# Starting the four TensorE lanes of a convolution loop one step apart instead of two

## The chip, the cores and the metric

One core of one Trainium2 chip runs the whole program. The metric is the device time of one execution in microseconds. All instructions are issued by hand on five engines: TensorE (PE in the profile, with its weight loads as PEld), VectorE (DVE), ScalarE (ACT), GpSimd (POOL) and SyncE (SP), which only starts transfers. Engines wait for each other by semaphores.

## The reference, cut to what matters

```python
# x: (32, 128, 2048) float32; cond_128: (32, 128)
def cond_1x1(x, embedding, ...):            # L0, L2 and L3
    att = softmax(mlp(embedding))           # 8 weights per batch element
    agg_w = einsum('bk,koi->boi', att, weight[..., 0])
    return einsum('boi,bih->boh', agg_w, x) + (att @ bias_k)[:, :, None]

def conv(x, c, weight, c_weight, bias):     # L1: 9 taps, 4 groups of 32 channels
    out = lax.conv_general_dilated(x, weight, (1,), [(4, 4)], feature_group_count=4, ...)
    return out + einsum('nd,od->no', c, c_weight)[:, :, None] + bias[None, :, None]

x = x + cond_1x1(x, cond_128, L0...)
x = x + conv(x, cond_128, L1..., fside_S_0)
x = x + cond_1x1(x, cond_128, L2...)
x = x + cond_1x1(x, cond_128, L3...)
```

## The kernel before, in words

The first 39 us prepare, for each of the 32 batch elements, one 128x128 matrix for L0 plus the identity, and one for the product of L2 and L3. The loop over the batch elements is then three stages, each with float32 data split in a high and a low part, so that every product is made of three matmuls (high by high, low by high, high by low):

- layer 0 (`layer0_steps`, matmuls at L479): x times the L0 matrix, into the four PSUM banks of `aux_ps`. ScalarE makes the high part of the result (`x1_hi`, L610), VectorE the low part (`x1_lo`, L767).
- the convolution (`conv_steps`, L499): into the four PSUM banks of `cv_ps`. ScalarE makes `x2_hi` (L618) and VectorE `x2_lo` (L776).
- the output product (`out_steps`, L522): into `aux_ps` again. ScalarE adds the bias and writes `y_all` (L628), and SyncE stores it.

VectorE also splits the next input (L758 and L751), GpSimd splits the next matrices (L693, L703). VectorE's order in a turn of the loop is x2_lo of the last element, x1_lo of the next, then the input split. ScalarE's is x2_hi, x1_hi, y.

Each stage exists four times, once for each group g of 32 rows of TensorE's array, and each copy writes a bank of its own. A lane is such a copy: lane g runs all stages of all elements with operands of the 32 partitions `rows(g)`. A step is one matmul of 32x512 of each lane. Layer 0 and the output product take 12 steps each in a lane, the convolution 36, so a turn of the loop is 60 steps or 240 matmuls. In a lane, a turn n is: layer 0 of element n+1 (12 steps), 18 steps of the convolution of n, the output product of n-1 (12 steps), the last 18 steps of the convolution of n. `in_turn` takes one matmul from each lane in the order 0, 1, 2, 3 and writes them in that one order into TensorE's queue. `LAG` is the number of steps by which each lane starts after the one ahead of it:

```python
def lane(g):
    for _ in range(LAG * g):
        yield
    ...
    for _ in range(LAST_WAIT - LAG * g):
        yield
    yield from out_steps(B - 1, g)
```

Before, lanes 1, 2 and 3 are 2, 4 and 6 steps behind lane 0. `LAST_WAIT` (5) holds lane 0 back ahead of the last output product, which needs all four lanes' results of the last convolution.

The waits that matter for the change stand at the start of each stage. `conv_steps(n, g)` (L493, L494) waits until VectorE has finished the `x1_lo` of all four lanes of element n, and until it has finished with this lane's own convolution bank, `x2_lo` of element n-1 in bank g. `out_steps(n, p)` (L511 to L518) waits for `x2_lo` of all four banks and for `x1_lo` of n+2 in bank p. `layer0_steps` (L470 to L477) waits for the split matrices, the split input and for y to have left bank p. A lane's bank of `cv_ps` is thus free between the end of one convolution and the start of the next only for the 12 steps of layer 0 between them, and in that time ScalarE and then VectorE have to read it.

Of the kernel before, what the change touches and what calls it, by code (L numbers as in the profile page):

```python
# [37 lines left out]
PER = PH // HALVES  # L38
YBUFS = 4
CONV_A = 18  # L40
LAG = 2
LAST_WAIT = 5


# [25 lines left out]
def cond_resid_kernel(nc, x, net, consts, mix, bias, conv, c_weight, w3, out):  # L70
    with ExitStack() as ctx:  # L71
# [304 lines left out]
        def _(pe):  # L376
# [132 lines left out]
            def out_steps(n, p):  # L509

                pe.wait_ge(m_split, 2 * (n + 1))  # L511
                pe.wait_ge(x2_lo_done, PH * (n + 1))


                if n + 2 < B:
                    pe.wait_ge(x1_lo_done, PH * (n + 2) + p + 1)
                elif n + 2 == B:
                    pe.wait_ge(y_out, PH * (n - 1) + p + 1)  # L518
                i, steps = 0, 3 * G
                for g in range(G):  # L520
                    for w, a in ((m_hi, x2_hi), (m_lo, x2_hi), (m_hi, x2_lo)):
                        mm = pe.matmul(out_bank(n, p), w[n % 2][rows(p), g, :], a[n % 2][rows(p), g, :],  # L522
                                       start=(i == 0), stop=(i == steps - 1))
                        i += 1
                        if i == steps:
                            mm.then_inc(y_done, 1)
# [6 lines that stand above are left out]
# [10 lines left out]
                yield from out_steps(B - 2, g)  # L543
                for _ in range(LAST_WAIT - LAG * g):
                    yield
# [368 lines left out]
```

## Time and profile before

| | us |
|---|---|
| median of 3 runs | 491.51 |
| lowest, highest | 489.49, 498.12 |
| the profiled execution's own time | 491.17 |
| its span in the profile | 489.0 |
| mean granted TensorE clock | 0.997 of full |

The span goes from the first to the last instruction of the profiled execution; its own time is 2.17 us longer. TensorE is busy for 478.8 us of the span, VectorE for 327.0, ScalarE for 252.7 and GpSimd for 150.8. The ends of matmuls in the profile are modelled, so the start of a matmul and the start of the ScalarE instruction that reads its bank are the firmer numbers.

### The profile page before, as it was taken

To read this page: it belongs to the slowest core of one execution; us is meant where nothing else is said; L and a number is where in the kernel's file an instruction comes from. 1 tells how busy PE (TensorE), PEld (TensorE's weight loads), DVE (VectorE), ACT (ScalarE), POOL (GpSimd) and SP (SyncE) were. 2 spreads that over 40 slices of the span, in tenths; PEclk is the share of its full clock that TensorE was granted. 3 is DMA by queue.
4 is the path that set the end of the run, shared out by engine and by line. 5 is a ranking of instruction groups with operands and counts; after the bars stand their busy time and mean duration, and the time that the engine had idled before them with its cause. 6 is when DMAs were issued, how large, how long until landed. Compare 5 with 4: busy or idle time off the path is not lost.

```text
span 489.0 us, 17826 instructions
## 1 busy us (share of the span) xinstructions
PE 478.8 (98%) x7953; PEld 475.4 (97%) x7953; DVE 327.0 (67%) x416; ACT 252.7 (52%) x417; POOL 150.8 (31%) x149
## 2 busy tenths in 40 slices
PE   6999999999999999999999999999999999999995
PEld 5989999999999999999999999999999999999995
DVE  3857767766687676666787676768777676777423
ACT  4654455544454555444554555445545554455435
POOL 3832441424332241433223141333143143330110
PEclk9999999999999999999999999999999999999998
DMA  8397996566657666564656656565767756552224
GB/s 264 139 311 205 320 269 217 163 205 164 186 158 212 218 214 214 166 201 129 184 194 217 215 184 204 130 207 155 217 208 216 211 157 198 146 184 64 88 88 172
DMA packets 39099, 92.84 MB, mean 190 GB/s; under 512 B 4584, under 2 KB 25584, under 8 KB 35056
## 3 DMA queue, kind: packets, MB, share of 16 engines
q1 hardware_dynamic: 39024, 91.71, 60.3%
q8 instruction: 63, 1.03, 0.9%
q14 instruction: 12, 0.10, 0.1%
HBM read 53.93 MB, written 37.77 MB: 188 GB/s over the span
## 4 chain that ended last, share of the span: by engine, by line
PE 95%; DVE 2%; DMA 1%; ACT 1%; SPq 0%; DVEq 0%; issue 0%; POOL 0%
PE cv_ps L499 56%; PE aux_ps L479 18%; PE aux_ps L522 17%; PE cv_ps L424 2%; DMA consts_sb<-in_consts_dram 1%; DVE x_lo L751 1%; PE aux_ps L424 1%; PE cv_ps L522 1%; DVE shares L796 1%; ACT x_hi L610 0%; DVE x_lo L767 0%; DVEq L71 0%; PE cv_ps L459 0%; ACT x_hi L601 0%; PE aux_ps L396 0%
## 5 line engine op out<-in xcount | busy, mean ns | idle before, releaser
L499 PE MATMUL cv_ps<-x_hi,conv_lo 32*128 32x512 f32 x1536 | 327.8, 391 | 0.0
L499 PE MATMUL cv_ps<-x_hi,conv_hi 32*128 32x512 f32 x1536 | 327.2, 389 | 0.0
L499 PE MATMUL cv_ps<-x_lo,conv_hi 32*128 32x512 f32 x1536 | 327.1, 391 | 0.0
L499 PEld LDWEIGHTS cv_ps<-x_hi,conv_lo 32*128 32x128 f32 x1536 | 240.4, 183 | 0.2 <-issue 0.2
L499 PEld LDWEIGHTS cv_ps<-x_lo,conv_hi 32*128 32x128 f32 x1536 | 240.2, 184 | 0.1
L499 PEld LDWEIGHTS cv_ps<-x_hi,conv_hi 32*128 32x128 f32 x1536 | 239.0, 183 | 0.0
L776 DVE SCALAR_TENSOR_TENSOR x_lo<-cv_ps,d_all,x_hi 128x512 fp32r<-128x512 f32 x128 | 87.2, 744 | 132.4 <-ACT x_hi L618 132.4
L628 ACT ACTIVATE y_all<-aux_ps,e_all 128x512 f32<-128x512 f32 x124 | 75.2, 690 | 134.4 <-PE aux_ps L522 134.4
L479 PE MATMUL aux_ps<-x_hi,a_hi 32*128 32x512 f32 x512 | 116.6, 391 | 0.5 <-DVE x_lo L751 0.5
L479 PE MATMUL aux_ps<-x_lo,a_hi 32*128 32x512 f32 x512 | 116.6, 389 | 0.0
L479 PE MATMUL aux_ps<-x_hi,a_lo 32*128 32x512 f32 x512 | 116.5, 388 | 0.0
L522 PE MATMUL aux_ps<-x_hi,m_hi 32*128 32x512 f32 x496 | 115.0, 387 | 0.0
L522 PE MATMUL aux_ps<-x_hi,m_lo 32*128 32x512 f32 x496 | 114.5, 387 | 0.0
L522 PE MATMUL aux_ps<-x_lo,m_hi 32*128 32x512 f32 x496 | 113.9, 384 | 0.0
L618 ACT ACTIVATE x_hi<-cv_ps,d_all 128x512 fp32r<-128x512 f32 x128 | 77.8, 687 | 66.7 <-PE cv_ps L499 66.7
L751 DVE TENSOR_TENSOR x_lo<-x_sb,x_hi 128x1024 fp32r<-128x1024 f32 x64 | 89.1, 1396 | 2.9 <-ACT x_hi L601 0.9
L767 DVE SCALAR_TENSOR_TENSOR x_lo<-aux_ps,c_all,x_hi 128x512 fp32r<-128x512 f32 x128 | 87.4, 746 | 4.8 <-ACT x_hi L610 2.9
L610 ACT ACTIVATE x_hi<-aux_ps,c_all 128x512 fp32r<-128x512 f32 x128 | 77.8, 691 | 18.1 <-PE aux_ps L479 18.1
L693 POOL CAST a_hi<-a_rep 128x512 fp32r<-128x512 f32 x32 | 24.4, 764 | 191.3 <-DMA a_rep<-a_pairs 126.3
L479 PEld LDWEIGHTS aux_ps<-x_hi,a_hi 32*128 32x128 f32 x512 | 78.6, 183 | 0.8 <-issue 0.6
L479 PEld LDWEIGHTS aux_ps<-x_hi,a_lo 32*128 32x128 f32 x512 | 78.8, 184 | 0.1
L479 PEld LDWEIGHTS aux_ps<-x_lo,a_hi 32*128 32x128 f32 x512 | 78.5, 183 | 0.2
(123 smaller groups left out, 538.1 us busy)
## 6 DMA issues: line engine op xcount, KB each, us to landing
x_sb<-in_x_dram SPq DMA_DIRECT2D x31, 1024.0 KB, 6.6
out_dram<-y_all SPq DMA_DIRECT2D x62, 512.0 KB, 7.4
a_rep<-a_pairs SPq DMA_DIRECT2D x64, 128.0 KB, 7.5
m_rep<-m_pairs SPq DMA_DIRECT2D x64, 128.0 KB, 7.0
a_pairs<-a_all SPq DMA_DIRECT2D x1, 1920.0 KB, 12.4
m_pairs<-m_all SPq DMA_DIRECT2D x1, 1792.0 KB, 12.6
m_all<-in_mix_dram SPq DMA_DIRECT2D x3, 512.0 KB, 5.2
x_sb<-in_x_dram SPq DMA_DIRECT2D x2, 512.0 KB, 7.5
```

Source lines behind the costliest of these rows:

```text
L424: mm = pe.matmul(mix_bank(n, h)[:, B * HO * i:B * HO * (i + 1)], w[half_rows(h), ROUND * j + i, :], a[half_rows(h)].rearrange("p b o -> p ...
L479: mm = pe.matmul(aux_ps[:, p, :], w[n % 2][rows(p), g, :], a[h][rows(p), g % PER, :], start=(i == 0), stop=(i == steps - 1))
L499: mm = pe.matmul(cv_ps[:, g, :], w[rows(g), j, :], a[n % 2][rows(g), q, s:s + T], start=(i == 0), stop=(i == steps - 1))
L522: mm = pe.matmul(out_bank(n, p), w[n % 2][rows(p), g, :], a[n % 2][rows(p), g, :], start=(i == 0), stop=(i == steps - 1))
L610: nc.scalar.activation(x1_hi[n % 2][:, p, 1:T + 1], aux_ps[:, p, :], ACT.Identity, bias=c0_all[:, n:n + 1]).then_inc(x1_hi_done, 1)
L618: nc.scalar.activation(x2_hi[n % 2][:, g, :], cv_ps[:, g, :], ACT.Identity, bias=d_all[:, g, n:n + 1]).then_inc(x2_hi_done, 1)
L628: nc.scalar.activation(y_all[:, k % YBUFS, p % PER, :], bank[:, p, :], ACT.Identity, bias=e_all[:, n:n + 1]).then_inc(y_out, 1)
L693: nc.gpsimd.tensor_copy(a0_hi[n % 2][:], src).then_inc(a0_split, 1)
L751: nc.vector.tensor_tensor(x_lo[h][:], x_sb[n % 2][:, PER * h:PER * (h + 1)], x_hi[h][:].bitcast(F32), ALU.subtract).then_inc(x_lo_done, 1)
L767: nc.vector.scalar_tensor_tensor(x1_lo[n % 2][:, p, 1:T + 1], aux_ps[:, p, :], c0_all[:, n:n + 1], x1_hi[n % 2][:, p, 1:T + 1].bitcast(F32 ...
L776: nc.vector.scalar_tensor_tensor(x2_lo[n % 2][:, g, :], cv_ps[:, g, :], d_all[:, g, n:n + 1], x2_hi[n % 2][:, g, :].bitcast(F32), ALU.add, ...
L796: nc.vector.tensor_scalar(shares[:], lexp[:].unsqueeze(1).unsqueeze(3).to_broadcast([NB, 2, K, HO]), linv[:], None, ALU.mult).then_inc(sha ...
```

## The change

`LAG` goes from 2 to 1. Lanes 1, 2 and 3 start 1, 2 and 3 steps after lane 0. No instruction is added or removed, no tile changes its size, and all waits have the same semaphores and values. The order of TensorE's queue is different, because matmuls of other lanes now stand beside each other. The order on the other engines is as it was. The waiting ahead of the last output product (`LAST_WAIT - LAG * g`) was 5, 3, 1 and 0 steps and is 5, 4, 3 and 2, so that lane 3 begins it in step with the others and no longer one step later.

```diff
-LAG = 2
+LAG = 1
```

TensorE's queue where the lanes go from layer 0 to the convolution of element 1, before. The row with `[waits x2_lo_done,x1_lo_done]` is the first convolution matmul of a lane; the first row here is that of lane 2 and the last that of lane 3.

```order
342 L499 MATMUL cv_ps<-x_hi,conv_hi 128x512 [waits x2_lo_done,x1_lo_done]
343 L479 MATMUL aux_ps<-x_hi,a_lo 128x512
344 L499 MATMUL cv_ps<-x_lo,conv_hi 128x512
345 L499 MATMUL cv_ps<-x_hi,conv_hi 128x512
346 L499 MATMUL cv_ps<-x_hi,conv_lo 128x512
347 L479 MATMUL aux_ps<-x_lo,a_hi 128x512
348 L499 MATMUL cv_ps<-x_hi,conv_hi 128x512
349 L499 MATMUL cv_ps<-x_hi,conv_lo 128x512
350 L499 MATMUL cv_ps<-x_lo,conv_hi 128x512
351 L499 MATMUL cv_ps<-x_hi,conv_hi 128x512 [waits x2_lo_done,x1_lo_done]
```

The same place of TensorE's queue now, with the first convolution matmuls of lanes 0, 1 and 2.

```order
331 L499 MATMUL cv_ps<-x_hi,conv_hi 128x512 [waits x2_lo_done,x1_lo_done]
332 L479 MATMUL aux_ps<-x_lo,a_hi 128x512
333 L479 MATMUL aux_ps<-x_hi,a_lo 128x512
334 L479 MATMUL aux_ps<-x_hi,a_hi 128x512
335 L499 MATMUL cv_ps<-x_hi,conv_lo 128x512
336 L499 MATMUL cv_ps<-x_hi,conv_hi 128x512 [waits x2_lo_done,x1_lo_done]
337 L479 MATMUL aux_ps<-x_lo,a_hi 128x512
338 L479 MATMUL aux_ps<-x_hi,a_lo 128x512
339 L499 MATMUL cv_ps<-x_lo,conv_hi 128x512
340 L499 MATMUL cv_ps<-x_hi,conv_lo 128x512
341 L499 MATMUL cv_ps<-x_hi,conv_hi 128x512 [waits x2_lo_done,x1_lo_done]
```

From one lane's first convolution matmul to the next lane's there were 9 places in the queue (two steps of four, and one), and now there are 5 (one step of four, and one).

## Rows read from the trace of the kernel before

**Rows 1.** Page, part 1: engine, busy us (share of the span), instructions.
```profile
PE 478.8 (98%) x7953; PEld 475.4 (97%) x7953; DVE 327.0 (67%) x416; ACT 252.7 (52%) x417; POOL 150.8 (31%) x149
```

**Rows 2.** Page, part 4: the chain that ended last, by engine.
```profile
PE 95%; DVE 2%; DMA 1%; ACT 1%; SPq 0%; DVEq 0%; issue 0%; POOL 0%
```

**Rows 3.** Waits of PE, all: line waited for, us in total, times, longest us.
```profile
PE aux_ps L396 <- DVE shares L796: 2.3, 1, 2.3
PE cv_ps L406 <- DVE idle_sb L786: 1.2, 1, 1.2
PE aux_ps L382 <- DMA m_rep<-in_net_dram: 0.8, 1, 0.8
PE aux_ps L479 <- DVE x_lo L751: 0.5, 1, 0.5
PE cv_ps L457 <- DVE c_att L826: 0.4, 1, 0.4
```

**Rows 4.** Timeline of DVE, 260 to 275 us: start, us, what [idle before <-releaser].
```profile
260.27 2.73 DVE L776 SCALAR_TENSOR_TENSOR x_lo<-cv_ps,d_all,x_hi 128x512 fp32r<-128x512 f32 x4 [3.29 <-ACT x_hi L618]
...
274.20 2.73 DVE L776 SCALAR_TENSOR_TENSOR x_lo<-cv_ps,d_all,x_hi 128x512 fp32r<-128x512 f32 x4 [4.47 <-ACT x_hi L618]
276.99 2.73 DVE L767 SCALAR_TENSOR_TENSOR x_lo<-aux_ps,c_all,x_hi 128x512 fp32r<-128x512 f32 x4
```

**Rows 5.** Timeline of ACT, 273 to 280 us.
```profile
273.48 2.42 ACT L618 ACTIVATE x_hi<-cv_ps,d_all 128x512 fp32r<-128x512 f32 x4 [1.68 <-PE cv_ps L499]
276.27 2.42 ACT L610 ACTIVATE x_hi<-aux_ps,c_all 128x512 fp32r<-128x512 f32 x4 [0.37 <-PE aux_ps L479]
```

**Rows 6.** Timeline of PE, 273.0 to 273.3 us: lane 0 ends its convolution.
```profile
273.04 0.39 PE L499 MATMUL cv_ps<-x_lo,conv_hi 32*128 32x512 f32 x1
...
273.27 0.39 PE L479 MATMUL aux_ps<-x_hi,a_hi 32*128 32x512 f32 x1
```

**Rows 7.** Timeline of PE, 276.0 to 277.7 us: first convolution matmul of lanes 0 and 3.
```profile
276.05 0.39 PE L499 MATMUL cv_ps<-x_hi,conv_hi 32*128 32x512 f32 x1
...
277.45 0.39 PE L479 MATMUL aux_ps<-x_lo,a_hi 32*128 32x512 f32 x1
...
277.68 0.39 PE L499 MATMUL cv_ps<-x_hi,conv_hi 32*128 32x512 f32 x1
```

**Rows 8.** Timeline of PEld, 277.2 to 277.5 us: weight loads of lane 3.
```profile
277.22 0.18 PEld L479 LDWEIGHTS aux_ps<-x_lo,a_hi 32*128 32x128 f32 x1
...
277.45 0.18 PEld L499 LDWEIGHTS cv_ps<-x_hi,conv_hi 32*128 32x128 f32 x1
```

**Rows 9.** Line 67 (semaphore waits) in 276.9 to 277.1 us: duration ns, first and last start.
```profile
L67 PEldq EVENT_SEMAPHORE  x1: 51/51/51, 277.0 to 277.0; - x1
```

**Rows 10.** Timeline of DVE, 51 to 54 us: the first turn.
```profile
51.37 2.73 DVE L776 SCALAR_TENSOR_TENSOR x_lo<-cv_ps,d_all,x_hi 128x512 fp32r<-128x512 f32 x4 [1.77 <-ACT x_hi L618]
```

**Rows 11.** Timeline of all engines, 54.1 to 54.4 us: loads and matmuls there.
```profile
54.02 0.39 PE L479 MATMUL aux_ps<-x_lo,a_hi 32*128 32x512 f32 x1
...
54.21 0.18 PEld L499 LDWEIGHTS cv_ps<-x_hi,conv_hi 32*128 32x128 f32 x1
54.24 0.18 PEld L499 LDWEIGHTS cv_ps<-x_lo,conv_hi 32*128 32x128 f32 x1
54.25 0.20 PEld L499 LDWEIGHTS cv_ps<-x_hi,conv_hi 32*128 32x128 f32 x2
54.25 0.46 PE L499 MATMUL cv_ps<-x_hi,conv_hi 32*128 32x512 f32 x1
54.26 0.39 PE L499 MATMUL cv_ps<-x_lo,conv_hi 32*128 32x512 f32 x1
```

**Rows 12.** Chain that ended last, 37 to 42 us; then PEld's and PE's timeline.
```profile
37.79 1.14 DVE x_lo L751
38.93 0.14 issue
...
39.03 0.18 PEld L479 LDWEIGHTS aux_ps<-x_hi,a_hi 32*128 32x128 f32 x1 [0.64 <-issue]
...
39.06 0.47 PE L479 MATMUL aux_ps<-x_hi,a_hi 32*128 32x512 f32 x1 [0.47 <-DVE x_lo L751]
```

**Rows 13.** Timeline of PE and of DVE at the end, from 483.1 us.
```profile
483.15 0.57 PE L522 MATMUL cv_ps<-x_lo,m_hi 32*128 32x512 f32 x3
483.37 0.38 PE L522 MATMUL cv_ps<-x_hi,m_lo 32*128 32x512 f32 x1
483.59 0.38 PE L522 MATMUL cv_ps<-x_lo,m_hi 32*128 32x512 f32 x1
...
483.73 1.41 DVE L848 TENSOR_SCALAR y_all<-cv_ps,e_all 128x512 f32<-128x512 f32 x2 [3.38 <-PE cv_ps L522]
```

## The prediction

> **What bounds the kernel now.** I read the engines' busy times first, then the chain that ended last, then TensorE's waits, and then one turn of the loop engine by engine. TensorE is busy for 98% of the span and the next engine, VectorE, for 67% [rows 1]. The chain lies on TensorE for 95% [rows 2]. Of TensorE's five waits none is of a convolution matmul (L499) or of an output matmul (L522); the only one of a loop line, L479, is that for the first split input, once, 0.5 us [rows 3]. So inside the loop TensorE's array waits for nobody.
>
> The period of a turn is the distance of two groups of x2_lo on VectorE: 274.20 - 260.27 = 13.93 us [rows 4]. A turn is 60 steps, so a step takes 0.232 us. A lane alone needs nearly as much: at the very end lane 3's last two matmuls, with no other lane left, start at 483.37 and 483.59 [rows 13]. A lane's weight load starts where its previous matmul starts (both at 277.45), and its matmul follows 0.23 us later, at 277.68 [rows 7, 8]. A lane is bound by its own sequence of load and matmul, and four lanes together cost what one costs. With 31 such turns, the question is how far each wait is from being one.
>
> **How much room the waits have.** The tightest is that of `conv_steps` for its own bank. Lane 0's last convolution matmul starts at 273.04, and its layer 0 one step later, at 273.27 [rows 6]. Call 273.04 the lane's end. ScalarE starts x2_hi 0.44 us after it, at 273.48, and has done all four banks at 275.90 [rows 5]. VectorE starts x2_lo at 274.20 and is done with the fourth bank, that of lane 3, at 276.93 [rows 4]: 3.89 us after lane 0's end.
>
> Lane 0 starts its next convolution at 276.05, 13 steps after its end (3.01 us). Lane 3 starts it at 277.68, 1.63 us later, which is its six steps of lag (1.39 us) and its place within a step (0.23 us) [rows 7]. So it comes 0.75 us after its bank is free. The semaphore instruction of the wait ends at about 277.0, right behind VectorE's end and 0.4 us ahead of the load at 277.45 [rows 9, 8]: TensorE's queue already stands at this wait and is let go by VectorE, while the array still works off what was handed to it before. The wait is live, but hidden.
>
> How much of the 0.75 us is needed is seen where TensorE is nearly late. In the first turn VectorE ends lane 3's bank at 54.10 (51.37 + 2.73) [rows 10]. The load of a first convolution matmul starts at 54.21, and its matmul is recorded at 54.25 with a length of 0.46 us, where the others have 0.39: it got going 0.07 us late, at 54.32, 0.22 us after VectorE's end [rows 11]. The wait for the first input says the same: VectorE ends at 38.93, the load starts at 39.03, and a matmul of 0.47 us is recorded at 39.06, so it runs from 39.14, 0.21 us after [rows 12]. I take 0.23 us, and as bounds 0.19 us (half the matmul's lateness left out) and 0.33 us (0.11 to the load, its whole 0.18, and 0.04 for three other loads behind it). Of the 0.75 us, 0.52 is spare (0.42 to 0.56).
>
> **The change part by part.** Nothing is added or removed; only the distance of the lanes changes.
>
> *Term 1, the wait for lane 3's bank.* Lane 3 comes three steps less behind lane 0: 3 x 0.232 = 0.70 us. What releases it does not come earlier, because that chain begins at lane 0's end and goes at VectorE's own pace: four x2_lo take 2.73 us, 0.66 us apart, while the lanes' ends will lie about 0.25 to 0.30 apart. ScalarE does not become the bound: its four take 2.42 us, so the fourth x2_hi is ready 2.86 us after lane 0's end, and VectorE's fourth x2_lo starts 3.15 us after it. So the bank is free after 3.89, and the matmul may run at 3.89 + 0.23 = 4.12. It is due at 3.01 + 0.70 + 0.23 = 3.94. It is late by 0.18 us, or 0.70 less the spare; the bounds are 0.14 and 0.28.
>
> *Who stands behind it.* TensorE has one queue, and while it stands at lane 3's wait nothing behind is handed on: the next matmul of lane 0, then of lanes 1 and 2. Lane 0's next is due 17 steps after its end, 17 x 0.232 = 3.94 us, at the same time as lane 3's first, and is late by the same. This closes the circle: from lane 0's end over ScalarE and VectorE to lane 0's own 17th matmul takes 4.12 us in place of 3.94, then follow 43 steps to its next end. The loss is paid anew in each turn: a period of 4.12 + 43 x 0.232 = 14.10 us.
>
> By the Trainium skill (TensorE: Matmul & The Clock Gate, The mechanism) weight loads can be pulled ahead of running matmuls while matmuls start in program order. A lane behind the wait could then not fill the gap, as in the forecast; the first turn's rows agree in that the loads that follow the late one come right behind it, at 54.24 and 54.25 [rows 11].
>
> *Lanes 0 to 2.* VectorE frees their banks 1.98, 1.32 and 0.66 us before lane 3's, that is 1.91, 2.57 and 3.23 us after lane 0's end. With 0.23 added they may start at 2.14, 2.80 and 3.46, and are due at 3.01 and later (one and two steps, 3.24 and 3.47, at the least). None is late, lane 2 by a hair.
>
> *How often.* The wait stands ahead of the convolutions of elements 1 to 31: 31 x 0.18 = 5.6 us; with the bounds 4.3 to 8.7 us. In the first of them lane 3 has no spare left even now; it could lose up to 0.70 instead of 0.18, 0.5 us once. I put that into the range.
>
> *Term 2, start and end.* At the start lanes 1 to 3 begin earlier, but lane 0's chain is as long as before and sets the turns: 0. At the end lane 3 no longer starts its last product a step after the others. VectorE evacuates lanes 1 and 3 there as a pair, 1.41 us for both from 483.73 [rows 13]: the second can't start before about 484.4, later than lane 3's end of 483.59 + 0.38 = 483.97. So the step saves nothing, and at most 0.23.
>
> *Everything else.* The output product waits for x1_lo of its bank. That group starts at 276.99 [rows 4] and ends, at the same 2.73 us, at 279.72. Lane 3's output product starts 18 steps (4.18 us) after 277.68, at 281.86: 2.1 us of room, of which three steps take 0.7. Input, split matrices and stores hang on whole turns.
>
> A rule bears on the latency. The trace has 0.10 to 0.11 us from VectorE's end to the weight load [rows 10 to 12]. The Trainium skill (Advanced Engine Details and Errata, Network/Comms) gives 50 to 100 ns for reading a semaphore from a sequencer. By its lower end the estimated loss would be 0.05 to 0.06 us a turn smaller, some 1.7 us in all, and the time about 495; no row here is that short.
>
> *Sum.* 491.17 (the profiled execution's own time: span 489.0 and 2.17 around it) + 5.6 + 0 = 496.8 us. The profiled execution is 0.34 us below the median of the runs shown, too little to matter. That is 1.1% slower. About 2% (9.8 us) is what a measurement of this kernel can tell from no change; 0.317 us a turn would reach it.
>
> **The rivals.**
>
> *A dearer restart (slower by over 2%).* When lane 3's wait ends, all four lanes have run dry and load weights anew. If they come out spread wider, the loss is the wait and part of a step more. Price: from the 0.07 us of the late matmul [rows 11] to a step, 0.23: 31 x 0.07 to 31 x 0.23 is 2.2 to 7.1 us more, 499.0 to 503.9 us. It decides the verdict from 0.14 us a turn on (501.1). Against it: lanes 1 and 2 were due later within the step than lane 0, so they have room to absorb a spread.
>
> *The wait is absorbed (no change).* The array works off what was handed to it, and a queue that runs far ahead could hide 0.18 us. Price: 491.2 us. Against it: what is behind the wait can't be handed over, and lane 0's next matmul is due within a step of lane 3's first. For it: only that the bounds of the latency rest on two rows.
>
> *Closer lanes run faster (not slower than before).* Steps take 0.232 us in the loop, but 0.22 in the last rows, with output matmuls alone (483.15, 483.37, 483.59) [rows 13]. With lanes closer together more steps hold matmuls of one stage only. Were all 43 steps behind the wait 0.227 us long, the period would be 4.12 + 9.76 = 13.88 us, and the time 491.2 - 31 x 0.05 = 489.6 us. It wins over the wait once steps fall by 0.18 / 43 = 0.004 us. Against it: 36 of 60 steps are convolutions anyway.
>
> **How the numbers follow.** The forecast has a chance of 0.70, the dearer restart 0.12 (half of it above 2%), the absorbed wait 0.11, the faster lanes 0.07. The forecast's own range is 495.4 to 499.9. With part of the restart's cases and part of those in which the wait is hidden or won back, the range that should hold the time 8 times in 10 is 493.0 to 500.3. Slower by over 2%: 0.07. Faster by over 2% needs 481.7 us, which no case gives: 0.01. Within 2%: 0.92.
>
> **What would show it.** The distance of two x2_lo groups on VectorE should be 14.11 us instead of 13.93, the group itself still 2.73 us. The semaphore instruction of lane 3's wait should again end right behind VectorE's end, but the load should follow at 0.11 us instead of 0.5, and lane 0's 17th matmul should run 4.1 us after its end in every turn. Steps elsewhere should stay at 0.232. The prediction is wrong if VectorE's group gets longer, if the period stays at 13.93, if another lane or stage is late, or if the period grows by clearly more than lane 3's lateness.

## The result and the profile after

The changed kernel takes 496.14 us (median of 6 runs, 495.15 to 497.80), the kernel before 491.77 (6 runs, 489.49 to 498.12). The ratio is 1.0096, 95% interval 1.0063 to 1.0130: about 1% slower, clear of noise, and within 2%. The prediction was 496.8 us, range 493.0 to 500.3.

| | before | after |
|---|---|---|
| span of the profiled execution | 489.0 | 494.9 |
| its own time | 491.17 | 497.80 |
| TensorE busy, share of the span | 478.8, 98% | 484.1, 98% |
| weight loads busy, share of the span | 475.4, 97% | 454.5, 92% |

The first row of the page's part 1 after, to be held against [rows 1]:

```profile
PE 484.1 (98%) x7953; PEld 454.5 (92%) x7953; DVE 327.2 (66%) x416; ACT 252.2 (51%) x417; POOL 153.4 (31%) x149
```

TensorE's share of busy time is 98% in both. The share of the bound engine is a poor witness here, because a matmul that starts late is recorded as a long one. The weight loads, which are recorded with their own ends, fall from 97% to 92%, but most of that is no standing still either. Their idle time grows by 26.8 us (from 489.0 - 475.4 to 494.9 - 454.5), and the gaps at the wait are 10.0 us of it. In the rest of a turn the lanes now load nearly at the same moment, which leaves a little time in each step in which none loads: from 284 to 288 us, with no wait in it, loads cover 3.65 of 4.00 us.

The timeline of VectorE after, two turns of the loop, answers to [rows 4]:

```profile
262.98 2.73 DVE L776 SCALAR_TENSOR_TENSOR x_lo<-cv_ps,d_all,x_hi 128x512 fp32r<-128x512 f32 x4 [3.40 <-ACT x_hi L618]
...
277.09 2.73 DVE L776 SCALAR_TENSOR_TENSOR x_lo<-cv_ps,d_all,x_hi 128x512 fp32r<-128x512 f32 x4 [4.88 <-ACT x_hi L618]
```

The period is 277.09 - 262.98 = 14.11 us, 0.18 more than the 13.93 before, and the group of four x2_lo is still 2.73 us long. The next three timelines are of the turn that begins at 276 us: TensorE where lane 0 ends its convolution, ScalarE (as [rows 5]), and the weight loads with the matmuls at the wait for lane 3's bank (as [rows 7, 8, 11]).

```profile
275.94 0.39 PE L499 MATMUL cv_ps<-x_lo,conv_hi 32*128 32x512 f32 x1
...
276.17 0.39 PE L479 MATMUL aux_ps<-x_hi,a_hi 32*128 32x512 f32 x1
```

```profile
276.37 2.42 ACT L618 ACTIVATE x_hi<-cv_ps,d_all 128x512 fp32r<-128x512 f32 x4 [1.72 <-PE cv_ps L499]
```

```profile
279.93 0.18 PEld L499 LDWEIGHTS cv_ps<-x_hi,conv_hi 32*128 32x128 f32 x1 [0.33 <-issue]
279.96 0.18 PEld L499 LDWEIGHTS cv_ps<-x_hi,conv_lo 32*128 32x128 f32 x1
279.97 0.18 PEld L499 LDWEIGHTS cv_ps<-x_hi,conv_hi 32*128 32x128 f32 x1
279.97 0.18 PEld L499 LDWEIGHTS cv_ps<-x_lo,conv_hi 32*128 32x128 f32 x1
```

```profile
279.64 0.39 PE L499 MATMUL cv_ps<-x_hi,conv_lo 32*128 32x512 f32 x1
279.65 0.39 PE L499 MATMUL cv_ps<-x_hi,conv_hi 32*128 32x512 f32 x1
279.65 0.39 PE L499 MATMUL cv_ps<-x_lo,conv_hi 32*128 32x512 f32 x1
279.96 0.47 PE L499 MATMUL cv_ps<-x_hi,conv_hi 32*128 32x512 f32 x1
279.96 0.49 PE L499 MATMUL cv_ps<-x_hi,conv_lo 32*128 32x512 f32 x1
279.97 0.49 PE L499 MATMUL cv_ps<-x_hi,conv_hi 32*128 32x512 f32 x1
279.97 0.50 PE L499 MATMUL cv_ps<-x_lo,conv_hi 32*128 32x512 f32 x1
```

Lane 0's end is 275.94. ScalarE starts 0.43 us after it, VectorE at 277.09, and VectorE ends lane 3's bank at 279.82, 3.88 us after lane 0's end. The load follows 0.11 us later, at 279.93, where it was 0.5 us before the change. In the gap of 0.33 us no lane loads anything. Then all four lanes load within 0.04 us. Their matmuls are recorded as starting within 0.01 us, 0.47 to 0.50 us long instead of 0.39. Taking the surplus off, they run from 280.04 to 280.08, about 4.12 us after lane 0's end, as forecast. That is the change: once in each turn the array runs dry.

The list of waits names it weakly. Of TensorE's weight loads after:

```profile
PEld cv_ps L499 <- issue: 10.0, 31, 0.4
```

31 gaps, one for each convolution from element 1 to 31, 0.32 us each in the mean. The releaser is given as "issue", not as VectorE, probably because the wait instruction itself stands between VectorE's end and the load. And 10.0 us of gap is not 10.0 us of loss: a little of it is there without a wait (the next loads were due at 279.64, where the lanes' previous matmuls start), and a load that starts late still has some room before its matmul is due. So the period grew by 0.18 and not by 0.33.

### The profile page after: what moved, and what is told of

The parts are those of the page before. It is cut to its first block, busy times and chain, and to the rows that moved or that the text cites. A ratio compares the mean times of both kernels' runs of the same rounds, so it can differ in the third digit from the quotient of the medians.

```text
span 494.9 us, 17826 instructions
## 1 busy us (share of the span) xinstructions
PE 484.1 (98%) x7953; PEld 454.5 (92%) x7953; DVE 327.2 (66%) x416; ACT 252.2 (51%) x417; POOL 153.4 (31%) x149
## 4 chain that ended last, share of the span: by engine, by line
PE 95%; DVE 2%; DMA 1%; ACT 1%; SPq 0%; DVEq 0%; issue 0%; POOL 0%
PE cv_ps L499 57%; PE aux_ps L479 18%; PE aux_ps L522 16%; PE cv_ps L424 2%; DMA consts_sb<-in_consts_dram 1%; DVE x_lo L751 1%; PE aux_ps L424 1%; PE cv_ps L522 1%; DVE shares L796 0%; ACT x_hi L610 0%; DVE x_lo L767 0%; DVEq L71 0%; PE cv_ps L459 0%; ACT x_hi L601 0%; PE aux_ps L396 0%
## 5 line engine op out<-in xcount | busy, mean ns | idle before, releaser
L499 PE MATMUL cv_ps<-x_hi,conv_hi 32*128 32x512 f32 x1536 | 307.7, 393 | 0.0
L499 PE MATMUL cv_ps<-x_hi,conv_lo 32*128 32x512 f32 x1536 | 307.7, 392 | 0.0
L499 PE MATMUL cv_ps<-x_lo,conv_hi 32*128 32x512 f32 x1536 | 307.3, 393 | 0.0
L499 PEld LDWEIGHTS cv_ps<-x_hi,conv_lo 32*128 32x128 f32 x1536 | 230.9, 184 | 3.4
L479 PE MATMUL aux_ps<-x_hi,a_hi 32*128 32x512 f32 x512 | 104.1, 391 | 0.5 <-DVE x_lo L751 0.5
L479 PE MATMUL aux_ps<-x_lo,a_hi 32*128 32x512 f32 x512 | 104.5, 389 | 0.0
L479 PE MATMUL aux_ps<-x_hi,a_lo 32*128 32x512 f32 x512 | 103.8, 388 | 0.0
L522 PE MATMUL aux_ps<-x_hi,m_hi 32*128 32x512 f32 x496 | 102.4, 387 | 0.0
L522 PE MATMUL aux_ps<-x_hi,m_lo 32*128 32x512 f32 x496 | 102.1, 387 | 0.0
L522 PE MATMUL aux_ps<-x_lo,m_hi 32*128 32x512 f32 x496 | 101.9, 384 | 0.0
```

Source lines behind the costliest of these rows:

```text
L479: mm = pe.matmul(aux_ps[:, p, :], w[n % 2][rows(p), g, :], a[h][rows(p), g % PER, :], start=(i == 0), stop=(i == steps - 1))
L499: mm = pe.matmul(cv_ps[:, g, :], w[rows(g), j, :], a[n % 2][rows(g), q, s:s + T], start=(i == 0), stop=(i == steps - 1))
```

## The experiments

The bank theory is the prediction's: a turn costs max(13.93, time until lane g's bank is free and its matmul can run, plus the steps left). The rivals are that lanes suffer from running close together (by contention, or by a bad restart), that the distance of neighbouring lanes counts, and that the room of 0.52 us is not there or is of another size. Periods are the median distance of two x2_hi groups on ScalarE over 27 turns of the profiled execution: 13.935 us before and 14.118 after. The kernel before was run beside each group of experiments (medians 490.52, 491.43 and 491.42 us).

In some of these profiled executions single turns are longer for another reason, and the spans must not be compared. The second turn of the run with lags 0, 1, 2 and 4 takes 15.72 us, with 1.86 us in which TensorE loads nothing and no releaser is recorded; with lags 0, 3, 3, 3, with the extra instruction (full and half) and with the shorter group there are turns 0.6 to 0.8 us too long. The profiles before and after have none. The cause was not looked into. The median period leaves such turns out.

**Lanes 0, 1, 2 and 4 steps behind.** This and the other tables of lags replace the product `LAG * g`:

```diff
-LAG = 2
+LAGS = (0, 1, 2, 4)
-    for _ in range(LAG * g):
+    for _ in range(LAGS[g]):
-    for _ in range(LAST_WAIT - LAG * g):
+    for _ in range(LAST_WAIT - LAGS[g]):
```

> Lanes start 0, 1, 2 and 4 steps after lane 0 (the changed kernel has 0, 1, 2, 3). Bank theory: only lane 3's first convolution matmul is late in the changed kernel. With one step more it is due 3.01 + 0.93 + 0.23 = 4.17 us after lane 0's end, its bank is ready at 4.12, so nothing is late: period 13.93 us, time 491.5 (491 to 492.5). Closeness theory (the lanes are slower because they run close together, or restart badly): lanes 0 to 2 are as close as in the changed kernel, so most of the 0.18 us a turn stays: 495 to 496.

Measured 491.51 us (490.06 to 494.76), ratio to before 1.0022 (0.9995 to 1.0049), period 13.932 us. One step more for lane 3 alone gives back the whole loss, although lanes 0 to 2 are as close as in the changed kernel. The closeness theory falls. VectorE's timeline shows the period (275.84 to 289.79; turns alternate by 0.02 to 0.03):

```profile
275.84 2.73 DVE L776 SCALAR_TENSOR_TENSOR x_lo<-cv_ps,d_all,x_hi 128x512 fp32r<-128x512 f32 x4 [4.68 <-ACT x_hi L618]
...
289.79 2.73 DVE L776 SCALAR_TENSOR_TENSOR x_lo<-cv_ps,d_all,x_hi 128x512 fp32r<-128x512 f32 x4 [3.32 <-ACT x_hi L618]
```

**Lanes 0, 3, 3 and 3 steps behind.**

```diff
-LAG = 2
+LAGS = (0, 3, 3, 3)
```

> Lanes 1, 2 and 3 all start 3 steps after lane 0. Bank theory: only lane 3's distance to lane 0 counts, and it is the same as in the changed kernel: period 14.11 us, time 496.1 (495.5 to 497). Theory that the distance of neighbouring lanes counts: lanes 1 to 3 are now in the same step, lane 0 is further off, so the period moves away from 14.11 by 0.1 us or more, to either side: under 494 or over 499.

Measured 497.02 us (496.11 to 498.71), ratio 1.0136 (1.0100 to 1.0171), period 14.162 us. It lies within 0.05 us of the changed kernel's, so lane 3's distance to lane 0 decides, and not that of neighbouring lanes. The 0.04 us more has its place too:

```profile
277.29 2.77 DVE L776 SCALAR_TENSOR_TENSOR x_lo<-cv_ps,d_all,x_hi 128x512 fp32r<-128x512 f32 x4 [4.86 <-ACT x_hi L618]
```

VectorE's group is 2.77 instead of 2.73 us long, because lane 1 now ends three steps after lane 0 and VectorE's second instruction waits a little for it.

**No lag.**

```diff
-LAG = 2
+LAG = 0
```

> All four lanes in the same step. Bank theory: lane 0's next matmul behind lane 3's wait is due 14 steps (3.25 us) after its end and can run at 4.12, late by 0.87 us a turn: period 14.80 us, and 31 x 0.87 = 27 us over 491.2, so 518 (516 to 520). Linear theory (0.18 us for each step of lag taken away): the period goes up by 0.36 in all, 502. Closeness theory: little more than the changed kernel, 497 to 500.

Measured 518.58 us (516.91 to 519.42), ratio 1.0567 (1.0532 to 1.0602), period 14.818 us against 14.80 expected. The loss is not linear in the lag: 0 from lag 2, 0.18 us a turn at lag 1, and 0.88 at lag 0, that is 0.70 more for three steps of 0.23. A threshold and then the full price. Here the gap is so long that the list of TensorE's waits names the right pair, with only the last 0.2 us of each:

```profile
PE cv_ps L499 <- DVE x_lo L776: 6.0, 31, 0.2
```

**The kernel before, with one more VectorE instruction.** It reads bank 2 and writes a tile that nobody reads; the computation is unchanged.

```diff
+        spare = sb("spare", [P, 2, T], F32R)
 ...
                     dve.wait_ge(x2_hi_done, PH * n + g + 1)
+                    if g == 2:
+                        nc.vector.scalar_tensor_tensor(spare[:, n % 2, 0:T], cv_ps[:, g, 0:T],
+                                                       d_all[:, g, n:n + 1],
+                                                       x2_hi[n % 2][:, g, 0:T].bitcast(F32), ALU.add,
+                                                       ALU.subtract)
```

> The kernel before (lag 2) with one more VectorE instruction of 128x512 ahead of lane 2's x2_lo, into a tile that nobody reads. It makes VectorE's group 0.66 us longer (3.39 instead of 2.73). Bank theory: of it 0.52 us is spare, 0.14 us a turn is paid: period 14.07, 491.5 + 4.3 = 495.8 (494.5 to 497). If the room that I read (0.52 us) is not there: up to 0.66 a turn, 512. If the wait is hidden by a queue that runs far ahead: 491.5.

Measured 495.55 us (494.57 to 496.82), ratio 1.0111 (1.0075 to 1.0146), period 14.072 us.

```profile
275.15 1.41 DVE L782 SCALAR_TENSOR_TENSOR x_lo<-cv_ps,d_all,x_hi 128x512 fp32r<-128x512 f32 x2 [4.33 <-ACT x_hi L619]
276.48 0.74 DVE L778 SCALAR_TENSOR_TENSOR spare<-cv_ps,d_all,x_hi 128x512 fp32r<-128x512 f32 x1
277.14 1.40 DVE L782 SCALAR_TENSOR_TENSOR x_lo<-cv_ps,d_all,x_hi 128x512 fp32r<-128x512 f32 x2
```

The group now ends at 278.54, 3.39 us after it began instead of 2.73. Of the 0.66 us added, 14.07 - 13.93 = 0.14 are paid. If every microsecond past the room is paid in full, as the run with lag 1 and the full instruction shows below, the room of the kernel before is 0.52 us: the prediction's number, which rests on its reading of two late matmuls.

**The same with half an instruction** (`0:T // 2` in place of `0:T`).

> The kernel before (lag 2) with one more VectorE instruction of 128x256 ahead of lane 2's x2_lo, into a tile that nobody reads. It should make the group some 0.39 us longer, less than the 0.52 us of room. Bank theory: period 13.93, 491.5 (491 to 492.5). If every lengthening of VectorE's group is paid: 31 x 0.39 = 12 us, 503.6.

Measured 492.68 us (median of 10). One of the ten, the profiled one, took 791.99 us at a mean granted clock of 0.56 (the last section tells of it); without it the ratio is 1.0029 (0.9999 to 1.0060). That fits the bank theory and not the price of 12 us. For a trace at the usual clock the kernel was profiled once more:

> The same kernel as in the half-instruction experiment, for a trace at the usual clock. Bank theory: VectorE's group is 3.0 to 3.2 us long, the period is still 13.93 us, and the load of lane 3's first convolution matmul comes 0.1 to 0.2 us after VectorE's end, close to the 0.11 us where it would begin to cost. Otherwise the period is 13.93 plus what the group has grown.

One run, 492.19 us, period 13.926 us. The group:

```profile
273.82 1.41 DVE L782 SCALAR_TENSOR_TENSOR x_lo<-cv_ps,d_all,x_hi 128x512 fp32r<-128x512 f32 x2 [4.45 <-ACT x_hi L619]
275.15 0.47 DVE L778 SCALAR_TENSOR_TENSOR spare<-cv_ps,d_all,x_hi 128x256 fp32r<-128x256 f32 x1
275.54 1.40 DVE L782 SCALAR_TENSOR_TENSOR x_lo<-cv_ps,d_all,x_hi 128x512 fp32r<-128x512 f32 x2
```

It is 3.12 us long, 0.39 more than before, and free. Together with the full instruction this puts the threshold between 0.39 and 0.66 us. VectorE now ends lane 3's bank at 276.94, and the wait is no longer hidden as far as the load goes:

```profile
277.05 0.18 PEld L500 LDWEIGHTS cv_ps<-x_hi,conv_hi 32*128 32x128 f32 x1
```

```profile
276.97 0.39 PE L480 MATMUL aux_ps<-x_lo,a_hi 32*128 32x512 f32 x1
...
277.21 0.39 PE L500 MATMUL cv_ps<-x_hi,conv_hi 32*128 32x512 f32 x1
...
277.31 0.39 PE L500 MATMUL cv_ps<-x_hi,conv_lo 32*128 32x512 f32 x1
```

Lane 3's load starts 0.11 us after VectorE's end and 0.08 after the start of the lane's previous matmul (276.97), where it would otherwise start. Its matmul is on time all the same, at 277.21, one step after that. Lane 0's next is the one at 277.31. Its bound would be 276.94 + 0.23 = 277.17, so 0.14 us of room is left to it, as 0.52 - 0.39 says. Lane 3's own matmul had only 0.04 left: it stands 0.10 us ahead of lane 0's here, where the two were level before.

**The changed kernel with a shorter group.** Lane 2's x2_lo is made for 256 of its 512 columns; the other half of that low part is left out.

```diff
-LAG = 2
+LAG = 1
 ...
+                    w = T // 2 if g == 2 else T
-                    nc.vector.scalar_tensor_tensor(x2_lo[n % 2][:, g, :], cv_ps[:, g, :], d_all[:, g, n:n + 1],
+                    nc.vector.scalar_tensor_tensor(x2_lo[n % 2][:, g, 0:w], cv_ps[:, g, 0:w], d_all[:, g, n:n + 1],
 ...
```

> The changed kernel (lag 1) with lane 2's x2_lo cut to 256 of 512 columns, so the other half of that low part is left out of the computation. VectorE's group gets some 0.27 us shorter, more than the 0.18 us of lateness. Bank theory: period 13.93, 491.5 (491 to 492.5). Closeness theory: the lanes are as close as in the changed kernel, 496.

Measured 490.62 us (489.15 to 494.32), ratio to before 0.9985 (0.9956 to 1.0015), period 13.934 us.

```profile
273.80 2.48 DVE L777 SCALAR_TENSOR_TENSOR x_lo<-cv_ps,d_all,x_hi 128x512 fp32r<-128x512 f32 x4 [4.69 <-ACT x_hi L618]
```

The lanes are one step apart as in the changed kernel, and VectorE's group is 0.25 us shorter than 2.73, more than the 0.18 that was late. The loss is gone. So inside the loop it is the length of VectorE's chain that makes lag 1 slower, and not that the lanes are close. The weight loads are busy for 94% of the span here (461.0 us), although no turn waits: their fall with lag 1 is no measure of the waiting.

**Three steps apart** (`LAG = 3`).

> Lanes three steps apart. Bank theory: the wait has 0.70 us more room, which is worth nothing: period 13.93. At the end lane 3 begins its last product 4 steps after the others (9 steps of lag against LAST_WAIT of 5), up to 0.9 us: 491.5 to 492.5. If the kernel before still paid something for the nearness of its lanes, the period falls below 13.93 and the time below 490.5.

Measured 490.16 us (489.48 to 494.04), ratio 0.9983 (0.9957 to 1.0009), period 13.945 us. More lag buys nothing: the kernel before had already hidden all of the chain. The up to 0.9 us at the end that I had allowed for does not show in the time.

**The changed kernel with the full extra instruction.** The edit of the fourth experiment, with `LAG = 1`.

> The changed kernel (lag 1) with one more VectorE instruction of 128x512 ahead of lane 2's x2_lo, into a tile that nobody reads. Bank theory: there is no room left, so all of the 0.66 us is paid in each turn on top of the 0.18: period 14.77, 496.1 + 31 x 0.66 = 516.6 (515 to 518). If part of the loss were something else than VectorE's chain, less: under 512.

Measured 517.55 us (515.89 to 520.10), ratio 1.0536 (1.0482 to 1.0590), period 14.778 us against 14.77 expected. Past the threshold every 0.66 us that VectorE takes longer costs 0.66 us a turn.

**Lanes 0, 0, 0 and 4 steps behind.**

```diff
-LAG = 2
+LAGS = (0, 0, 0, 4)
```

> Lanes 0, 1 and 2 in the same step, lane 3 four steps behind (where it was never late in the experiment with 0, 1, 2, 4). Bank theory: now lane 2's bank is the late one. VectorE ends it at 3.23 us after lane 0's end, the matmuls behind it can run at 3.46, lane 0's next is due at step 14, 3.25: late by 0.21 us a turn, period 14.14, 490.8 + 31 x 0.21 = 497.3 (496 to 498.5). If only lane 3's distance could ever matter: 491.

Measured 497.53 us (497.14 to 501.82), ratio 1.0158 (1.0101 to 1.0214), period 14.163 us against 14.14 expected. The late bank is lane 2's now:

```profile
276.55 2.73 DVE L776 SCALAR_TENSOR_TENSOR x_lo<-cv_ps,d_all,x_hi 128x512 fp32r<-128x512 f32 x4 [4.93 <-ACT x_hi L618]
```

```profile
278.74 0.18 PEld L499 LDWEIGHTS cv_ps<-x_hi,conv_hi 32*128 32x128 f32 x1 [0.36 <-issue]
```

VectorE ends its group at 279.28 and lane 2's bank 0.66 us ahead of that, at 278.62. The load follows 0.12 us later, well before lane 3's bank is free. The same sum holds for another lane with its own numbers.

| | VectorE's group, us | period expected | period measured |
|---|---|---|---|
| before | 2.73 | | 13.935 |
| lag 1, the change | 2.73 | 14.11 | 14.118 |
| lags 0, 1, 2, 4 | 2.73 | 13.93 | 13.932 |
| lags 0, 3, 3, 3 | 2.77 | 14.11 | 14.162 |
| lag 0 | 2.73 | 14.80 | 14.818 |
| lag 2, full extra | 3.39 | 14.07 | 14.072 |
| lag 2, half extra | 3.12 | 13.93 | 13.926 |
| lag 1, short | 2.48 | 13.93 | 13.934 |
| lag 3 | 2.86 | 13.93 | 13.945 |
| lag 1, full extra | 3.39 | 14.77 | 14.778 |
| lags 0, 0, 0, 4 | 2.73 | 14.14 | 14.163 |

None of these beats the kernel before beyond its noise. The best of them differ from it by less than their intervals.

## Why the prediction was right

*The bound and the room.* The reading that the array waits for nobody while its queue already stands at the wait held. The room of 0.52 us is what the extra instruction measured (0.66 added, 0.14 paid). It is the room of lane 0's next matmul in the queue, though. The prediction took lane 3's place within the step, 0.23 us, as given; with the half instruction lane 3 came 0.10 us earlier in the step than lane 0, so its own room is not a fixed number. The period did not suffer from it. The latency of 0.23 us, taken from one matmul recorded 0.07 us too long and from the first one of the loop, came back in the turn shown: VectorE's end at 279.82, the matmuls from about 280.06, and the period says the same of all turns.

*Term 1.* Forecast late by 0.18 us a turn, measured 14.118 - 13.935 = 0.183. VectorE's group kept its length, ScalarE did not become the bound, and the closed circle over lane 0's own next matmul is seen in the four lanes that start as one at 279.96. Over all turns the distance from the first x2_lo group to the last grew from 426.26 us (51.37 to 477.63) to 432.08 (51.25 to 483.33), by 5.8 us, where the term was 5.6.

*The first turn.* I left a possible 0.5 us of it to the range. Its period grew by 0.30 us (13.89 to 14.19), so 0.12 more than an ordinary turn.

*Term 2.* Forecast 0, at most 0.23 saved. It went slightly the other way. From the last group on, the rest of the program takes 11.57 us (483.33 to 494.9) instead of 11.37 (477.63 to 489.0), 0.20 more. TensorE's timeline at the start of the last product shows a part of it:

```profile
486.21 0.85 PE L522 MATMUL cv_ps<-x_hi,m_hi 32*128 32x512 f32 x4
```

These are the first matmuls of the four lanes. From the first one's start to the last one's end it is 0.85 us, and one such late matmul is 0.47 us long, so they start 0.13 us apart, where a convolution's four lanes started within 0.01. The likely reason, which no run tests, is that the lanes pass their waits there one after the other, and now all four stand in the same step. Before, lane 3's stood one step later. What it costs in all was not measured by itself.

*The rivals.* The dearer restart was priced at 0.07 to 0.23 us a turn on top. The four lanes came out of the gap within 0.04 us of each other, and the period, 14.118 against 14.10 from the wait alone, has at most 0.02 us left over for it. The absorbed wait did not happen at lag 1. It is what happens at lag 2 with half an instruction more, where the load is late and its matmul is not. Faster steps of close lanes did not show either: with lags 0, 1, 2, 4 the period is 13.93 as before.

*The size.* The spans differ by 5.9 us (489.0 to 494.9), the medians by 4.4 (491.77 to 496.14). The kernel before alone spreads over 489.49 to 498.12, and I read the traces for the mechanism and the ratio for the size. By its interval the loss is 3.1 to 6.4 us, which holds the forecast of 5.6. That the median came within 0.7 us of 496.8 is partly luck, since the executions of one kernel differ by more than that. A slip in the prediction changes nothing: the lower end of the forecast's own range is 491.17 + 4.3 = 495.5, not 495.4.

## What to carry to other kernels

A wait that costs nothing has a distance to costing something. Add up the chain that releases it (here PSUM to ScalarE to VectorE to TensorE, 3.89 + 0.23 us) and the time until it is due (a count of steps times the pace), and the difference tells what a change of order, of lag or of an engine's work will do: nothing up to the threshold, and the full price for each turn behind it. Where several lanes share one in-order queue, one lane's wait stops all, and it is enough to move that lane alone.

## What the runs showed of the hardware that I had not expected

TensorE's queue runs well ahead of its array. In the kernel before, the semaphore instruction for lane 3's bank ends at about 277.0, right behind VectorE's end, and the lane's load follows 0.4 us later, in its turn. So the list of waits shows nothing, although in the turn that was read the queue did wait, and the array did not.

A matmul that starts late after a full stop is recorded early and long. After the gap the rows have 0.47 to 0.50 us instead of 0.39, and the busy share of TensorE stays at 98%. For such gaps the single rows of the weight loads are the better ones (0.33 us, from 279.60 to 279.93). Their share of the span is not: it falls from 97% to 92% with the change, but to 94% in the run with the shorter group too, which loses nothing. Whether the lanes' loads lie side by side or one after the other counts for more in it than the waits do.

One of the profiled executions, with half an extra instruction at lag 2, ran at little more than half of TensorE's clock nearly throughout and took 791.99 us. Its page:

```profile
PEclk9555555555555555555555555555555555555555
```

The granted clock is 1.00 up to 16 us, 0.56 from 16.5 us on, and 0.50 for a few microseconds (30 to 33 and 48 to 50 us); of the two levels, 2.4 and 1.2 GHz, these are at or near the lower one. TensorE was busy without a break from 12 us until the clock fell, and for 0.85 and 1.11 us of the two stretches 8 to 10 and 10 to 12 us. The same kernel in the later execution, with 0.75 and 1.33 us there, kept 1.00. A turn takes 23.06 us instead of 13.93, that is 0.384 us a step, while the loop's weight loads are 0.20 us in the mean instead of 0.18. So a step follows the clock although the load hardly does. The prediction had called a lane bound by its sequence of load and matmul; these rows say that it is mainly the matmul. The other nine executions took 490.16 to 495.19 us, eight of them at a mean granted clock of 0.995 or more and one at 0.950 (491.87 us). Nothing in the kernel differs between them, and what lowered the clock was not found out.
